# A sort of 400,000 graph edges: two-byte comparison matrices from written-out constants, and the value product on VectorE

## What is computed

```python
def _spmm(row, col, vals, x):
    msg = vals[:, None] * x[col]
    return jax.ops.segment_sum(msg, row, num_segments=N)

def _layer(x_prev, row, col, vals, W_a, b_a, W_b, b_b):
    h = _spmm(row, col, vals, x_prev)
    z = (h + x_prev) @ W_a.T + b_a + h * x_prev @ W_b.T + b_b
    return jnp.where(z >= 0, z, NEG_SLOPE * z)
```

## Time and profile before

| | |
|---|---|
| median of 3 runs | 9584.01 us |
| lowest and highest | 9575.98 and 9594.1 us |
| span of the profiled execution | 9617.6 us |
| busy, whole span | PE 91%, PEld 84%, DVE 81%, ACT 45%, POOL 53% |
| the sort's windows | from 238 us to 3180 us |

### The profile page before, as it was taken

One profiled execution on the slowest core, in us unless ns is written; L12 is line 12 of the kernel. 1 busy time (PEld: TensorE's weight loads), 2 busy tenths in 40 slices (PEclk: granted clock), 3 DMA queues, 4 the chain that ended last, 5 costly groups with the idle time before them and its releaser, 6 DMA issues.

```text
span 9617.6 us, 226010 instructions
## 1 busy us (share of the span) xinstructions
PE 8753.9 (91%) x69832; PEld 8044.4 (84%) x69833; DVE 7775.5 (81%) x11265; ACT 4351.4 (45%) x13668; POOL 5100.5 (53%) x2965
## 2 busy tenths in 40 slices
PE   7788886888888489989999999999999999999999
PEld 4577775577777389989999999999999999899999
DVE  7899998899999777777777777777777777777777
ACT  0677774277777245541111356531111555511112
POOL 8688885188888200018888300048888000078885
PEclk8788888888888699999999999999999999999999
DMA  2211111011111999998888799998888799988886
GB/s 82 34 6 6 6 6 18 8 6 6 6 6 6 32 274 338 336 316 285 286 287 285 211 335 340 331 302 287 286 287 285 232 332 340 324 285 286 287 285 207
DMA packets 1101073, 1893.75 MB, mean 197 GB/s; under 512 B 388436, under 2 KB 439704, under 8 KB 1100344
## 3 DMA queue, kind: packets, MB, share of 16 engines
q0 software_dynamic: 378656, 958.17, 33.5%
q1 hardware_dynamic: 595104, 926.26, 30.4%
q10 hardware_dynamic: 127224, 8.24, 3.3%
HBM read 1136.46 MB, written 755.66 MB: 197 GB/s over the span
## 4 chain that ended last, share of the span: by engine, by line
PE 47%; DVE 20%; DMA 18%; issue 9%; ACT 3%; SPq 1%; ACTq 1%; DVEq 0%; POOL 0%; POOLq 0%
PE ps L937 34%; DMA messages<-work 17%; DVE place L1102 7%; PE ps L928 6%; DVE hT L1123 4%; DVE hT L1118 3%; PE ps L775 3%; ACT work L699 3%; DVE place L1105 2%; DVE hT L1246 1%; PE ps L825 1%; PE ps L945 1%; PE ps L965 1%; PE ps L966 1%; DVE place L1107 0%
## 5 line engine op out<-in xcount | busy, mean ns | idle before, releaser
L533 POOL DMA_INDIRECT work<-messages,work x1776 | 2708.7, 1525 | 3618.6 <-issue 3617.3
L937 PE MATMUL ps<-work 128*128 128x125 f32 x28416 | 3282.6, 278 | 38.4 <-DVE work L1299 38.4
L937 PEld LDWEIGHTS ps<-work 128*128 128x128 f32 x28416 | 3242.8, 192 | 78.2 <-DVE work L1299 39.0
L928 PE MATMUL ps<-xb,work 125*128 x21504 | 2471.8, 277 | 185.9 <-DVE work L1271 110.6
L928 PEld LDWEIGHTS ps<-xb,work 125*128 125x128 f32 x21504 | 2429.4, 192 | 228.2 <-issue 225.1
L1299 DVE TENSOR_TENSOR work<-work,iota_p 128x1000 f32<-128x1000 f32 x1776 | 2121.7, 1195 | 35.8 <-ACT work L717 35.8
L699 ACT ACTIVATE work<-ps,work 128x128 f32<-128x128 f32 x5376 | 1506.0, 372 | 1254.4 <-DMA messages<-work 790.0
L499 POOL DMA_INDIRECT sorted_edges<-stage,run_idx x798 | 1605.1, 2011 | 472.7 <-ACT stage L630 246.9
L717 ACT ACTIVATE work<-work 128x8 f32<-128x8 f32 x1776 | 534.3, 301 | 2669.9 <-DMA work<-messages,work 2669.9
L825 PEld LDWEIGHTS ps<-hT 128*128 128x128 f32 x12768 | 1620.4, 208 | 97.9 <-issue 73.2
L825 PE MATMUL ps<-hT 128*128 128x96 f32 x12768 | 1600.2, 290 | 44.0 <-ACT stage L630 35.7
(11 more groups left out here) (205 smaller groups left out, 4087.1 us busy)
## 6 DMA issues: line engine op xcount, KB each, us to landing
messages<-work SPq DMA_DIRECT2D x2688, 256.0 KB, 6.4
work<-slot_cols SPq DMA_DIRECT2D x672, 256.0 KB, 6.3
work<-messages,work POOLq DMA_INDIRECT x1776, 5.9
out_x<-xb SPq DMA_DIRECT2D x150, 125.0 KB
sorted_edges<-stage,run_idx POOLq DMA_INDIRECT x798, 3.3
work<-lane_places SPq DMA_DIRECT2D x532, 5.2 KB
out_x<-xb ACTq DMA_DIRECT2D x4, 1562.5 KB
sorted_edges<-hT SPq DMA_DIRECT2D x4, 908.0 KB
```

Source lines behind the costliest of these rows:

```text
L533: pool.indirect_dma_start(out=ck[:, n, :, :].rearrange("p h x -> p (h x)"), out_offset=None, in_=flat, in_offset=bass.IndirectOffsetOnAxis ...
L928: last = t.matmul(ps[:, n % PR, j * D:(j + 1) * D], col_hot[:, n % OHR, j * P:(j + 1) * P], x_flat[:, bass.ds(offs[n], D)], start=True, st ...
L937: last = t.matmul(part[n], ck[:, n, j // CH, j % CH * D:(j % CH + 1) * D], sel[:, n % SELB, j, :], start=j == 0, stop=j == CHB - 1)
```

## The change

Three things are done in the sort, and the rest of the program is as before.

1. **Constants written out.** `iota_b` (100 numbers, read with repeats) becomes `iota_bl`, 100 x 24 two-byte numbers in which each is stored 24 times; `iota_s` (48 float32 numbers plus 8192) becomes `iota_cl`, 48 x 24 two-byte numbers. The offset of 8192 is taken off in the tables once for each pass instead.
2. **Two-byte in_slot with the lanes innermost.** `slot` goes to a two-byte buffer `slot_b`, and in_slot is stored as 48 slots by 24 lanes. Both inputs and the output of this comparison, and of one_hot, are now two-byte and step by one element. The products want the slots innermost and so read in_slot through the view `slot_of_lane`: 48 steps of 24 elements, which is 48 bytes from one element to the next.
3. **The value product moves from GpSimd to VectorE**, ahead of the packed product. GpSimd keeps only its transfers; the semaphore `valued_ready` is gone. VectorE's one_hot moves up to just behind the reduce, and its part of to_part ahead of in_slot.

```diff
-        iota_s = sb("iota_s", [P, SLOTS])
+        slot_b = sb("slot_b", [P, 2, LANES], BF16)
...
-        iota_b = sb("iota_b", [P, NB], BF16)
...
+        IB0 = IR0 + SPARE // 2
+        iota_bl = wb[:, 2 * IB0:2 * IB0 + OHW].rearrange("p (b l) -> p b l", l=LANES)
+        IC0 = IB0 + OHW // 2
+        iota_cl = wb[:, 2 * IC0:2 * IC0 + SLOTS * LANES].rearrange("p (c l) -> p c l", l=LANES)
...
-        in_slot = hT[:, IS0:IS0 + SLOTW].rearrange("p (l c) -> p l c", c=SLOTS)
+        in_slot = hb[:, 2 * IS0:2 * IS0 + SLOTW].rearrange("p (c l) -> p c l", l=LANES)
+        slot_of_lane = in_slot.rearrange("p c l -> p l c")
...
-            count(iota_s[:, :], [[1, SLOTS]], base_=int(BIG))
+            count(iota_cl, [[1, SLOTS], [0, LANES]])
...
-            count(iota_b[:, :], [[1, NB]])
+            count(iota_bl, [[1, NB], [0, LANES]])
...
-            def move_values(p, i, q):
-                n = WOFF[p] + i * 2 + q
-                pool.wait_ge(in_slot_ready, n + 1)
-                g.tensor_tensor(out=moved[q][:, :, 1, :], in0=in_slot,
-                                in1=value[p][:, bass.ds(i * (2 * LANES) + q * LANES, LANES)][:, :, None].to_broadcast([P, LANES, SLOTS]),
-                                op=ALU.mult).then_inc(valued_ready, 1)
...
-                def both(i, q):
-                    move_values(p, i + q, 1 - q)
-                    scatter(p, i, q, False)
-
-                pairs(pool, 1, half - 1, both)
+                pairs(pool, 1, half - 1, lambda i, q: scatter(p, i, q, False))
...
-                pe.wait_ge(valued_ready, n + 1)
...
-                link(v.tensor_tensor(tab("at"), tab("at"), tab("first"), ALU.subtract))
+                link(v.scalar_tensor_tensor(tab("at"), tab("at"), -BIG, tab("first"), ALU.add, ALU.subtract))
...
-                                       iota_b[:, :, None].to_broadcast([P, NB, LANES]), ALU.is_equal).then_inc(onehot_ready, 1)
+                                       iota_bl, ALU.is_equal).then_inc(onehot_ready, 1)
...
                 v.tensor_reduce(at, ps[:, 0:BANKS, 0:BANKW].rearrange("p k (b l) -> p l k b", l=LANES), AX.XY,
                                 ALU.max).then_inc(rank_read, 1)
+                if more:
+                    one_hot(p, w + 2, q)
                 dve.wait_ge(rank_read, n + 1)
-                v.tensor_scalar(raised, at, -(BIG + (SLOTS - 1) / 2), 1.0 / SLOTS, ALU.add, ALU.mult).then_inc(raised_link, 1)
+                v.tensor_scalar(raised, at, -(SLOTS - 1) / 2, 1.0 / SLOTS, ALU.add, ALU.mult).then_inc(raised_link, 1)
...
-                if more:
-                    one_hot(p, w + 2, q)
                 if not first:
                     dve.wait_ge(ordered, n - 1)
+                v.tensor_tensor(to_part[q][:, ACTL:LANES, :], part_of[:, ACTL:LANES][:, :, None].to_broadcast([P, LANES - ACTL, P]),
+                                iota_p[:, None, :].to_broadcast([P, LANES - ACTL, P]), ALU.is_equal)
                 dve.wait_ge(slot_link, n + 1)
                 if not (first and q == 0):
                     dve.wait_ge(moved_ready, n)
-                    dve.wait_ge(valued_ready, n)
-                v.tensor_tensor(in_slot, slot[:, :, None].to_broadcast([P, LANES, SLOTS]),
-                                iota_s[:, None, :].to_broadcast([P, LANES, SLOTS]), ALU.is_equal).then_inc(in_slot_ready, 1)
-                v.tensor_tensor(to_part[q][:, ACTL:LANES, :], part_of[:, ACTL:LANES][:, :, None].to_broadcast([P, LANES - ACTL, P]),
-                                iota_p[:, None, :].to_broadcast([P, LANES - ACTL, P]), ALU.is_equal)
+                v.tensor_tensor(in_slot, slot[:, None, :].to_broadcast([P, SLOTS, LANES]), iota_cl, ALU.is_equal).then_inc(in_slot_ready, 1)
                 dve.wait_ge(in_slot_ready, n + 1)
-                v.tensor_tensor(moved[q][:, :, 0, :], in_slot, packed[p][:, bass.ds(w * LANES, LANES)][:, :, None].to_broadcast([P, LANES, SLOTS]),
+                v.tensor_tensor(moved[q][:, 0:LANES, 1, :], slot_of_lane[:, 0:LANES, :],
+                                value[p][:, bass.ds(w * LANES, LANES)][:, :, None].to_broadcast([P, LANES, SLOTS]), ALU.mult)
+                v.tensor_tensor(moved[q][:, :, 0, :], slot_of_lane, packed[p][:, bass.ds(w * LANES, LANES)][:, :, None].to_broadcast([P, LANES, SLOTS]),
                                 ALU.mult).then_inc(moved_ready, 1)
```

More of the change, by code:

```diff
@@ L196, in graph_layers @@
         iota_run = wb[0:NBD, 2 * IR0:2 * IR0 + SPARE]
-        assert IR0 + SPARE <= 20560
+        IB0 = IR0 + SPARE // 2
+        iota_bl = wb[:, 2 * IB0:2 * IB0 + OHW].rearrange("p (b l) -> p b l", l=LANES)
+        IC0 = IB0 + OHW // 2
+        iota_cl = wb[:, 2 * IC0:2 * IC0 + SLOTS * LANES].rearrange("p (c l) -> p c l", l=LANES)
+        assert IC0 + SLOTS * LANES // 2 <= 20560
         hot = [hb[:, r * LT:(r + 1) * LT] for r in range(HR)]
@@ L207, in graph_layers @@
         IS0 = MV0 + 4 * SLOTW
-        in_slot = hT[:, IS0:IS0 + SLOTW].rearrange("p (l c) -> p l c", c=SLOTS)
-        assert IS0 + SLOTW <= ABODIES * ZC
+        in_slot = hb[:, 2 * IS0:2 * IS0 + SLOTW].rearrange("p (c l) -> p c l", l=LANES)
+        slot_of_lane = in_slot.rearrange("p c l -> p l c")
+        assert IS0 + SLOTW // 2 <= ABODIES * ZC
         zeros = hT[:, 12544 - 2000:12544 - 2000 + ZW]
@@ L311, in graph_layers @@
         moved_ready = sem("moved_ready")
-        valued_ready = sem("valued_ready")
         act_copies = sem("act_copies")
@@ L507, in _ @@
                 half = WINDOWS[p] // 2
-                move_values(p, 0, 0)
-                move_values(p, 0, 1)
                 scatter(p, 0, 0, True)
-                move_values(p, 1, 0)
                 scatter(p, 0, 1, True)
-                def both(i, q):
-                    move_values(p, i + q, 1 - q)
-                    scatter(p, i, q, False)
-                pairs(pool, 1, half - 1, both)
+                pairs(pool, 1, half - 1, lambda i, q: scatter(p, i, q, False))
                 scatter(p, half, 0, False)
@@ L1097, in window @@
                 n = WOFF[p] + w
-                at, raised, part_of, slot = [place[:, q, k, :] for k in range(4)]
+                at, raised, part_of = [place[:, q, k, :] for k in range(3)]
+                slot = slot_b[:, q, :]
                 dve.wait_ge(rank_ready, n + 1)
```

## The result

| | before | after |
|---|---|---|
| median | 9579.99 us (4 runs) | 9728.9 us (4 runs) |
| span of the profiled execution | 9617.6 us | 9738.7 us |
| ratio after / before | | 1.0154, 95% interval 1.0141 to 1.0167 |

The kernel became slower by 149 us. The direction was forecast and the time lies in the range (9640 to 10,300), but the forecast loss of 551 us is 3.7 times the real one; the number of the first rival ("the step costs half as much", 9712 us) is 17 us off.

What follows compares the result with a forecast made beforehand. VectorE's list of a 9.80 us sort window, 266 times, was taken as the bound. Terms -1.256 - 0.603 - 0.540 + 4.472 = +2.07 us a window, +551 us, gave 10,135 us; range 9640 to 10,300 us.

Steps and rivals of the forecast that it cites:

- the first rival: Products' stepped read of in_slot: extra only 0.69 ns per number, X 2.147 us, window +0.48 us, 9712 us; chance 0.31.
- What bounds the kernel: Sort windows: VectorE's instruction list, 9.80 us a window, 266 times; other engines have 1.1 to 2.0 us of room.
- One_hot at half the price: VectorE's one_hot, two-byte inputs in steps of one: 2659 to 1402 ns, -1.256 us a window.
- In_slot: VectorE's in_slot comparison, two-byte in steps of one: 1352 to 749 ns, -0.603 us a window.
- The stall of L1105: Small VectorE step held under GpSimd's product: mean 718 to 178 ns once GpSimd arithmetic goes, -0.540 us a window.
- The two products: VectorE's packed and value products reading in_slot in 48-byte steps: X 2.942 us each, +4.472 us a window.
- What costs nothing: Reordered one_hot and to_part, larger constants (some 4.5 us more on GpSimd, covered), GpSimd's lost work: no effect on time.
- The second: Products' stepped read free or below 0.48 ns extra: kernel faster, 9290 to 9340 us, say 9320; chance 0.16.
- The third (no doubling): One_hot and in_slot comparisons keep full price: 1.86 us a window come back, +495 us, 10,630 us; chance 0.06.
- The figure of the Trainium skill: Products' stepped read at 1.73 ns a column: X 2.14 us, the change costing about 0.5 us a window.
- break-even: Product duration at which the window stays unchanged: X of 1.906 us, an extra of 0.48 ns per number.
- the full price: Products' 48-byte steps cost 1.38 ns extra per number, as read at 96 bytes: 10,135 us; chance 0.47.

Runs made afterwards that it cites:

- one_hot alone: Kernel before with only the written-out two-byte constant for one_hot; in_slot float32, value product on GpSimd, old order: 9398.7 us (0.9808).
- the splits: Value product shared between VectorE and GpSimd: slots-innermost kernel, 12 VectorE lanes, 9363.47 us; in_slot stored in four-lane groups, 12 or 16 VectorE lanes, 9407.92 or 9407.29 us.
- the move alone: Kernel before with only the value product moved to VectorE, float32, slots innermost, steps of one: 9745.05 us (1.0171).
- the extras: Changed kernel with extra VectorE products ahead of the first sort, each at another step size: 2154 ns at 48 bytes, 3030 at 96 (two-byte or float32, within 3 ns).
- the kernel in fours: Changed kernel with in_slot stored in groups of four lanes, so the products read it in steps of 8 bytes: 9294.13 us (0.9704).

## Why the prediction was wrong, step by step

- **What bounds the kernel** (VectorE's list of a window, 266 times): right, before and after, and in every variant but those that load GpSimd (one_hot alone, the value product back on GpSimd, the splits) or TensorE. The same sum gave the times with steps of 96 and 64 bytes, with the slots innermost and with the move alone to within 0.5%.
- **One_hot at half the price**: forecast 1402 ns, measured 1399. Right.
- **In_slot**: forecast 749, measured 751. Right.
- **The stall of L1105**: forecast to go, from 718 to 178 ns; measured 173. Right.
- **The two products**: forecast X = 2.942 us, measured 2.200. This is the step that failed: "I take the price of the nearest two-input read, 1.38 ns". The mechanism, a step that is paid for, was right. The size was carried from a step of 96 bytes to one of 48, and 96 is a peak: the 1.38 ns is confirmed at 96 bytes (1.38 and 1.42 in the repeated form, 1.45 in the product's) and is 0.73 at 48 in the loop (0.69 in the extras; what the last 0.04 is was not found). With X = 2.200 the sum reads 2 x 2.200 - 1.412 - 2.399 = +0.589 us, 157 us, where the medians moved by 149.
- **What costs nothing**: right, within 0.03 us: with X = 2.200 the sum gives a window of 10.39 us and 10.42 was measured, the gap behind in_slot (0.15 us) included. The first reduce starts at 245.7 us as against 245.4, so the larger constants cost nothing.
- **The rivals**: the first one met the number, at 9712 us for a measured 9729, and not by its mechanism. It had half the price for half the distance, but 16 bytes cost 0.72 ns, 48 cost 0.69 and 64 cost 0.63. Its other source for 0.69 ns, the copy L1057, steps by 96 bytes and is another form of instruction. So the match with 0.73 is luck. The second, a step that costs nothing, was forecast at 9290 to 9340, and the kernel in fours, in which it does cost nothing, took 9294. The third (no doubling) did not occur.
- **The figure of the Trainium skill.** The Trainium skill ("Vector Engine (DVE) Microarchitecture Reference", section 5.2 "Measured stream behaviour on trn2") has 1.73 ns a column for one source that hops far at every element, hence the estimate of 2.14 us. By it the sum would have been +0.47 us a window, an estimate of some 125 us. The measurement is 2.15 to 2.20 us and 149. Its 2.50 for both sources, or the output alone, in steps of 24 words is what one source in steps of 96 bytes costs here, (3030 - 146) / 1152 = 2.50 ns. Its rule that the full rate holds only for adjacent pairs of words does not hold in these runs at 8 bytes: float32 numbers 8 bytes apart, no two of them adjacent, took 1357 ns, as in a row. The two figures together said that steps differ from each other; I set the row for one step above them both.
- **A slip in the working**: 19 us around break-even are 0.03 ns of the extra, not 0.04 (19 / 266 / 2 / 1152 us). It changes no chance.

The chances were off in one way as well: 0.47 for the full price against 0.31 for half. The one row at hand was for another step, and there was nothing in the trace that told 48 from 96 bytes; a forecast halfway, with both in the range, would have been what the rows allowed.

## What to carry to other kernels

A price taken from a row holds for that row's step and form; before it decides the sign or size of a sum, measure the very step in a handful of extra instructions. When one instruction wants an array one way and the next the other way, store it in groups small enough that the second one's step stays at 8 bytes; here both then ran at full rate. Work given to GpSimd is not free even under cover: here its product held VectorE back, and what paid was the first instruction behind the reduce, whether it had one tensor input (L1105) or two (one_hot), never the reduce itself, which reads PSUM and took 2.65 us in every window.

## What the hardware showed that was not expected

- The price of a stepped read on VectorE is not monotonic: 0 up to 8 bytes, 0.27 ns for each number at 12, 0.6 to 0.9 at most steps from 16 bytes on, 1.45 at 96, and every pair of sizes 256 bytes apart that was measured agrees. It is the same for two-byte and float32 numbers (within 6 ns at each size tried with both).
- Two two-byte inputs in runs of only four (with the row of the constant read again for each group) keep the half price: 751 ns for 1152 numbers.
- TensorE reading 96 float32 numbers in steps of 96 bytes begins a pass every 0.24 us, 2.5 ns for each number, at 1.2 and at 2.4 GHz alike; without the step it is 0.21 and 0.11 us. It is the price that VectorE pays at 96 bytes. The granted clock stood at 0.55 on average, with TensorE busy all the time.
